# First stage of a fused graph kernel: weights centred on ScalarE, bias rows padded to 128 rows, and the quad sums of eight edge chunks made by TensorE

## The reference, cut to what matters

```python
xn = _layernorm(x)
# graph branch: edges are sorted by destination
out1 = segment_sum(edge_attr, dst); cnt = segment_sum(1, dst)
out2 = segment_max(edge_attr, dst); out3 = out1 / max(cnt, 1)
h = relu(concat([xn, out1, out2, out3, u]) @ W1 + b1) @ W2 + b2 + xn
# mixer
q, k, v = split(xn @ W_qkv + b_qkv)
q = q - mean(q); k = k - mean(k)          # the kernel centres the weights instead
q2, k2 = normalised squares of q and k    # k2 is normalised over all nodes
attn = v + q2 @ (k2.T @ v) / sqrt(N);  m = attn @ W_out + b_out
x = x + h + m
# then: layer norm, top half of the rows by a router, gelu MLP on them, scatter back
```

## Time and profile before

| | us |
|---|---|
| median of 3 runs | 1256.93 |
| lowest and highest of them | 1256.19, 1265.18 |
| the profiled execution | 1254.3 |
| its span, first to last instruction | 1252.5 |
| busy in the span: PE, DVE | 1062.0 (85%), 1016.3 (81%) |
| busy in the span: ACT, POOL | 483.2 (39%), 478.6 (38%) |
| mean granted TensorE clock | 0.914 of 2.4 GHz |

### The profile page before, as it was taken

How to read it: one execution, slowest core, us unless ns; L and a number is a source line. 1 busy time by engine, 2 the same in 40 slices (tenths; PEclk the granted TensorE clock), 3 DMA queues, 4 the chain that set the end, 5 groups by cost and what they waited for, 6 DMA issues and landing times. The chain is left out here.

```text
span 1252.5 us, 15955 instructions
## 1 busy us (share of the span) xinstructions
PE 1062.0 (85%) x4570; PEld 766.4 (61%) x4570; DVE 1016.3 (81%) x2429; ACT 483.2 (39%) x1438; POOL 478.6 (38%) x344
## 2 busy tenths in 40 slices
PE   3198999999993668699999999999999613899997
PEld 1044545555541445378888888888888503677775
DVE  6999999999999999568888998888895476545552
ACT  3346676677751234122233332223333220422430
POOL 0078831888000004485444456544420040133311
PEclk9599999999997788589999999999999855799998
DMA  8789999999998799533333344333321120111100
GB/s 304 300 314 340 345 370 356 348 348 348 353 320 318 295 414 366 189 103 118 128 125 108 111 147 136 125 126 129 94 75 45 42 68 8 27 43 40 52 23 19
DMA packets 96013, 235.53 MB, mean 188 GB/s; under 512 B 13703, under 2 KB 68764, under 8 KB 89682
## 3 DMA queue, kind: packets, MB, share of 16 engines
q1 hardware_dynamic: 49890, 156.61, 34.1%
q10 hardware_dynamic: 31248, 44.71, 10.0%
q0 software_dynamic: 14816, 33.53, 9.4%
HBM read 154.25 MB, written 80.55 MB: 187 GB/s over the span
## 5 line engine op out<-in xcount | busy, mean ns | idle before, releaser
L366 POOL DMA_INDIRECT graw<-in_edge_attr,ic x98 | 144.6, 1476 | 74.8 <-DVE ob L809 39.2
L806 DVE SCALAR_TENSOR_TENSOR ob<-ob,mQ,mx 128x96 f32<-128x96 f32 x392 | 122.1, 312 | 4.7 <-issue 0.4
L809 DVE SCALAR_TENSOR_TENSOR ob<-ob,kQ,xb 128x96 f32<-128x96 f32 x392 | 121.7, 311 | 0.0
L509 POOL DMA_INDIRECT near<-ends_d,blki x49 | 89.2, 1821 | 76.9 <-DVEq L715 62.2
L509 POOL DMA_INDIRECT near<-in_dst,rowi x49 | 87.8, 1792 | 57.8 <-DVEq L724 43.1
L1458 PE MATMUL psQ<-Wqk,xT 128*128 128x512 f32 (+1 forms) x196 | 102.2, 646 | 0.0
L1367 ACT ACTIVATE hT_hi<-psQ 128x512 fp32r<-128x512 f32 (+1 forms) x52 | 29.7, 572 | 182.8 <-PE psQ L1657 182.8
L794 DVE TENSOR_TENSOR xb<-xb 128x1536 f32<-128x1536 f32 x49 | 86.2, 1758 | 1.7
L792 DVE TENSOR_TENSOR mx<-xb 128x1536 f32<-128x1536 f32 x49 | 85.5, 1745 | 0.9
L2007 POOL DMA_INDIRECT out_x<-zo,lst x25 | 24.4, 977 | 129.4 <-DVE zo L2054 129.4
L61 PE MATMUL psF<-F2w,gT_hi 128*128 128x512 f32 (+1 forms) x175 | 67.0, 418 | 0.0
(11 more groups left out here) (462 smaller groups left out, 3201.9 us busy)
## 6 DMA issues: line engine op xcount, KB each, us to landing
xb<-in_edge_attr SPq DMA_DIRECT2D x49, 1536.0 KB, 10.4
scan_d<-ob SPq DMA_DIRECT2D x49, 768.0 KB, 5.7
yrow_d<-yr SPq DMA_DIRECT2D x48, 132.0 KB
xg<-in_x ACTq DMA_DIRECT2D x12, 512.0 KB, 10.7
xT_d<-xT ACTq DMA_DIRECT2D x12, 512.0 KB
base_d<-dcur ACTq DMA_DIRECT2D x12, 512.0 KB
qT_d<-qT ACTq DMA_DIRECT2D x12, 512.0 KB, 10.1
out_x<-xres SPq DMA_DIRECT2D x48, 128.0 KB
```

The costliest lines, as they stand in the source:

```text
L366: nc.gpsimd.indirect_dma_start(out=to.rearrange("p i f -> p (i f)"), out_offset=None, in_=raw_v, in_offset=bass.IndirectOffsetOnAxis(ap=ic ...
L509: nc.gpsimd.indirect_dma_start(out=near[:, t, :], out_offset=None, in_=table, in_offset=bass.IndirectOffsetOnAxis(ap=rows[:, t:t + 1], axi ...
L806: nc.vector.scalar_tensor_tensor(o[:, q, 0:EF], prev[:, 0:EF], mQ[:, bass.ds(c * TQ + q, 1)], mx[:, q, 0, :], ALU.min, ALU.max).then_inc(s ...
L809: nc.vector.scalar_tensor_tensor(o[:, q, EF:AGG], prev[:, EF:AGG], kQ[:, bass.ds(c * TQ + q, 1)], X[:, q, 0, :], ALU.mult, ALU.add).then_i ...
```

## The change

In the first stage:

- ACT centres the weights and biases (6 passes with a sum, 6 with a bias), after its segment searches and ahead of the square root of the variances. DVE keeps only the splitting of the bias (`query_bias`), which now stands before `variances`; `bias_row` moves to just after chunk 0. ACT issues its two small DMAs before the square root.
- `bqs`, `brow` and `one_r` get 128 partitions, set to zero by POOL at the start, and the two bias matmuls of a tile run over all 128 rows.
- For chunks 1 to 4 and 36 to 39, PE makes the quad sums: for each half of a chunk (four quads) four matmuls with the identity add the four edges of each quad, 384 columns wide, in PSUM (`quad_sums`, 8 matmuls a chunk). DVE leaves out L794 and L797 there and reads the sums from PSUM; it waits for `s_ps` before each half. In PE's order, the sums of chunk 1 stand before the node turns, those of chunks 2, 3 and 4 after the base of tiles (0,1), (0,3) and (1,2) of the turns, those of 36 after the last turn, those of 37 after the matmuls that make `M`, and those of 38 and 39 after attention groups 0 and 2.
- The block of factors moves from after chunk 39 to after chunk 36, the ends of segments to after chunk 38, SP's weight loads by one chunk forward, and the table `NORM` gets new places. The starts of segments move behind attention group 3 and use `psKx`.
- At the end of the stage, the four tail parts stand together behind the transposes into `psR`, and ACT issues the six loads of the node stage before its casts of the tail.

```diff
+SUMS_EARLY = (1, 2, 3, 4)
+SUMS_LATE = (36, 37, 38, 39)
-            bqs = sb("bqs", [2, 2 * NF], f32r)
+            bqs = sb("bqs", [P, 2 * NF], f32r)
 (brow and one_r likewise)
-                with sp.Fori(0, 10) as g:
+                with sp.Fori(0, 9) as g:
...
-                    if c == 40:
+                    if c == 39:
                         sp.wait_ge(s_at, 6 + KF)
                         sp.wait_ge(s_fs, TILES)
-                    if c in (40, 41):
+                    if c in (39, 40):
...
+                for m in (bqs, brow, one_r):
+                    nc.gpsimd.memset(m[:, :].bitcast(f32), 0.0).then_inc(s_id, 1)
...
-                def centre_weights():
+                def query_bias():
+                    dve.wait_ge(s_cw, 12)
+                    dve.wait_ge(s_id, 9)
...
+                    on_pe = c in SUMS
                     nc.vector.tensor_tensor(mx, xp[..0..], xp[..1..], ALU.max)
+                    if not on_pe:
                         nc.vector.tensor_tensor(xp[..0..], xp[..0..], xp[..1..], ALU.add)
                     nc.vector.tensor_tensor(mx[:, :, 0, :], mx[:, :, 0, :], mx[:, :, 1, :], ALU.max)
+                    if not on_pe:
                         nc.vector.tensor_tensor(X[:, :, 0, :], X[:, :, 0, :], X[:, :, 2, :], ALU.add)
...
+                        if on_pe and q % 4 == 0:
+                            dve.wait_ge(s_ps, SUMS.index(c) * 2 + q // 4 + 1)
+                        quad_sum = psS[c][q // 4][:, q % 4 * EF:(q % 4 + 1) * EF] if on_pe else X[:, q, 0, :]
...
-                NORM = {5: 0, 7: 1, 10: 2, 13: 3, 16: 4, 18: 5, 21: 6, 24: 7, 26: 8, 29: 9, 32: 10, 34: 11, 35: 12}
+                NORM = {6: 0, 9: 1, 11: 2, 14: 3, 16: 4, 19: 5, 21: 6, 24: 7, 26: 8, 29: 9, 31: 10, 33: 11, 34: 12}
                 edge_chunk(0, 0, 0)
+                bias_row()
                 stats_quarter(1)
                 stats_quarter(2)
+                stats(GROUPS, 1, LAST, xs[0], s_xs[0], 64)
+                query_bias()
                 variances()
-                centre_weights()
-                bias_row()
                 deviations()
...
-                    if c == 39:
+                    if c == 36:
                         (factors kcol and rq, then s_fac)
-                    if c == 39:
+                    if c == 38:
                         ends_of_segments()
...
+                for w_, m_, o_ in centred:
+                    nc.scalar.activation(o_, w_, ACT.Copy, scale=-1.0 / NF, accum_out=m_).then_inc(s_cw, 1)
+                for i, (w_, m_, o_) in enumerate(centred):
+                    act.wait_ge(s_cw, i + 1)
+                    nc.scalar.activation(w_, w_, ACT.Identity, bias=m_).then_inc(s_cw, 1)
...
-                for g in range(GROUPS + 1):
+                for g in range(GROUPS):
                     attention_rows(g, g % 4, g // 4 * 16)
                     weights(g)
+                attention_rows(GROUPS, 0, GROUPS // 4 * 16)
                 (the six loads of the node stage)
+                weights(GROUPS)
...
+                def quad_sums(c):
+                    pe.wait_ge(s_load[c % XB], c // XB * 16 + 16)
+                    for h in range(2):
+                        if c not in (SUMS_EARLY[0], SUMS_LATE[0]):
+                            pe.wait_ge(s_sum, (c - 1) * TQ + 4 * h + 5)
+                        for i in range(4):
+                            ins = nc.tensor.matmul(psS[c][h][:, 0:4 * EF], ident[:, :], xb[c % XB][:, 4 * h:4 * h + 4, i, :],
+                                                   start=(i == 0), stop=(i == 3))
+                        ins.then_inc(s_ps, 1)
...
-                    nc.tensor.matmul(o, one_r[0:2, 0:rows], bqs[0:2, :], start=True, stop=False)
+                    nc.tensor.matmul(o, one_r[:, 0:rows], bqs[:, :], start=True, stop=False)
 (brow likewise)
...
+                        if (g, t) in ((0, 1), (0, 3), (1, 2)):
+                            quad_sums({(0, 1): 2, (0, 3): 3, (1, 2): 4}[g, t])
...
-                tail_part(0)
-                tail_part(1)
                 pe.wait_ge(s_scan, 2)
                 (transposes into psR)
-                tail_part(2)
-                tail_part(3)
+                for i in range(4):
+                    tail_part(i)
```

More of the change, by code:

```diff
@@ L349, in build @@
             psW = psQ + psKx
+            psS = {c: psKx if c in SUMS_EARLY else [psR, psC] for c in SUMS}
             psA, psH, psO = psT, psQ + psKx, [psR, psC]
@@ L738, in rows_to_gather @@
                     dve.wait_ge(s_t, 1)
-                    step(nc.vector.tensor_copy(Sbeg[:, :], psR[:, 0:TILES]))
+                    step(nc.vector.tensor_copy(Sbeg[:, :], psKx[1][:, 0:TILES]))
                     step(nc.vector.tensor_scalar(a1[:, :], Sbeg[:, :], 3.0, None, ALU.add), False)
@@ L1126, in _ @@
                 nc.scalar.copy(wrb[:, :], psKx[1][:, 0:NF + 1]).then_inc(s_wrb, 1)
+                act.wait_ge(s_wload, 16 * 8)
+                centred = [(Wqk[:, c, h * NF:(h + 1) * NF], wm[:, 2 * c + h:2 * c + h + 1], xn[2][:, 2 * c + h, 0:NF]) for c in range(KF) for h in range(2)]
+                centred += [(bqk[0:1, h * NF:(h + 1) * NF], wm[0:1, 4 + h:5 + h], xn[3][0:1, h, 0:NF]) for h in range(2)]
+                for w_, m_, o_ in centred:
[3 more added lines that the diff above has]
+                    nc.scalar.activation(w_, w_, ACT.Identity, bias=m_).then_inc(s_cw, 1)
+                act.wait_ge(s_bw, 2)
+                act.dma_start(brow[1:2, :].bitcast(f32), brow_l[0:1, :].bitcast(f32)).then_inc(s_row, 16)
+                act.wait_ge(s_wq, 1)
+                act.dma_start(bqs[1:2, :].bitcast(f32), bqs_l[0:1, :].bitcast(f32)).then_inc(s_row, 16)
                 act.wait_ge(s_ln, 1)
                 nc.scalar.sqrt(sd[:, :], va[:, :]).then_inc(s_sqrt, 1)
-                act.wait_ge(s_wq, 1)
-                act.dma_start(bqs[1:2, :].bitcast(f32), bqs_l[0:1, :].bitcast(f32)).then_inc(s_row, 16)
-                act.wait_ge(s_bw, 2)
-                act.dma_start(brow[1:2, :].bitcast(f32), brow_l[0:1, :].bitcast(f32)).then_inc(s_row, 16)
                 act.wait_ge(s_ln, 2)
@@ L1467, in base @@
                     o = psC[0:rows, 0:NF]
-                    nc.tensor.matmul(o, one_r[0:2, 0:rows], brow[0:2, :], start=True, stop=False)
+                    nc.tensor.matmul(o, one_r[:, 0:rows], brow[:, :], start=True, stop=False)
                     for c in range(KF):
@@ L1515, in _ @@
                 pe.wait_ge(s_wrb, 3)
+                quad_sums(1)
                 pe.wait_ge(s_wq, 1)
@@ L1542, in _ @@
                 ins.then_inc(s_pt, 1)
+                pe.wait_ge(s_at, 4)
+                quad_sums(SUMS_LATE[0])
                 pe.wait_ge(s_at, 5)
@@ L1557, in _, with starts_of_segments @@
                 ins.then_inc(s_pt, 1)
-                pe.wait_ge(s_end, 1)
-                nc.tensor.matmul(psR[:, 0:TILES], shift[:, :], Eend[:, :], start=True, stop=False)
-                nc.tensor.matmul(psR[:, 1:TILES], corner[:, :], Eend[:, 0:TILES - 1], start=False, stop=True).then_inc(s_t, 1)
+                quad_sums(SUMS_LATE[1])
                 pe.wait_ge(s_at, 6 + KF)
+                def starts_of_segments():
+                    pe.wait_ge(s_end, 1)
+                    nc.tensor.matmul(psKx[1][:, 0:TILES], shift[:, :], Eend[:, :], start=True, stop=False)
+                    nc.tensor.matmul(psKx[1][:, 1:TILES], corner[:, :], Eend[:, 0:TILES - 1], start=False, stop=True).then_inc(s_t, 1)
                 def low_part(i):
@@ L1569, in low_part @@
                     pe.wait_ge(s_min, 4)
+                    if i == 3:
+                        pe.wait_ge(s_idx, 1)
                     if i >= 4:
@@ L1605, in _ @@
                     attention(g, g % 4, g // 4 * 16 + 16)
+                    if g in (0, 2):
+                        quad_sums(SUMS_LATE[2 + g // 2])
+                    if g == 3:
+                        starts_of_segments()
                     weights(g)
```

64 lines of the change are left out of this document (23 added, 41 removed).

## The result

The changed kernel is slower: 1311.14 us (median of 4, 1310.66 to 1312.15) against 1260.41 for the kernel before beside it (1256.19 to 1265.18); the ratio is 1.0406, 95% interval 1.036 to 1.0452. The profiled execution took 1310.66 us, its span 1308.9. I had forecast 1271, at most 1281. Most of the difference is one stall, and it doesn't always come: further down the same kernel takes 1259.8 us on each of two chips.

The account below looks back on a forecast made before the run. DVE's unbroken edge scan was taken as the bound, PE a close second. 1254.3 + 16.4 (early and late waits) - 1.8 (end of stage) = 1268.9 us profiled, 1271 as median; range 1255 to 1281.

Parts of the forecast that it names:

- Where DVE then waits: Chunks 1 to 4: DVE waits for PE's place in the turns, some 28 us; chunk 4 ends at 106.9, before 91.8.
- the case to which I gave 0.42: Whole kernel: time the same as before, within about 1% (12.6 us); chance 0.42.
- PE reaches its quad sums sooner: Rival: first tile starts at 52, chunk 4 ends at 99.8, no late chunk waits; 1250 to 1261 us, chance 0.2.
- DVE's own work: Chunks with PE sums: 2.5 us shorter, eight times, 20 us; PSUM reads free; centring saves 4.25; chunk 1 starts at 51.3.
- when PE can begin: Chunk 1's sums on PE, first at half clock: halves at 54.3 and 57.2; node turns begin at 57.2.
- The waits of chunks 2 to 4: First carries wait on PE: halves at 68.5 and 71.3, 81.6 and 84.4, 102.1 and 105.0; some 13 us before chunk 4.
- The bias rows: Node tiles on PE: bias matmuls over 128 rows save 0.5 us a tile (0.4 to 0.6), leaving 3.55 us.
- the rival, no gain: Bias matmuls: padding saves nothing, a tile stays at 4.2 us; 1282 us (1277 to 1286), chance 0.17.
- The late four: Chunks 36 to 39: 36 without wait, 38 and 39 wait 2 and 6 us; 39 ends at 433.2, 16.4 later than before.
- The end of the stage: Tail and node-stage loads: `xTs_hi` starts 1.8 us earlier, at 522.4; 1.8 us gained (0 to 2.5).

Follow-up runs that it names:

- the control: The changed kernel unaltered, run on chip E beside two other versions: 1259.77 us, 1.0036 of the kernel before.
- two rows: The changed kernel with the bias matmuls over two rows again instead of 128, on chip E: 1269.25 us, 1.0125 of the kernel before.
- padding alone: The kernel before with only the bias rows padded to 128 rows, on chip B: 1254.22 us, 0.9982 of the kernel before.
- four others: Chip A: changed kernel without early sums 1247.41 us, with later gathers 1271.84, with two-row bias 1272.30; kernel before with DVE idled 1299.13.

## Why the prediction was wrong

The direction was right, the time was 40 us too low, and the runs show two errors that partly hide each other.

**The step that failed against the result** is "Where DVE then waits", in its chunk 3: "halves at 81.6, 84.4; ends at 86.3". By the records PE had them at 84.4 and 87.0 (that it began on them at 81.6 has to do with the late signals too: in the control without a stall it begins at 76.6), but DVE could use them only at 102.3 and 124.6. No term and no rival of the prediction has signals of PE that arrive late; the sum took it that work recorded as done releases its waiter, and nothing in the rows spoke against that. At chunk 5 it makes 49.7 us (152.7 against 103.0 in the control on chip E), which is nearly all of the 51 us between the two times.

**Where there is no stall**, the forecast of 1271 was 11 us too high, and 1.0036 is within 1%, the case to which I gave 0.42. The profiled control took 1260.5 against the 1268.9 of my sum; 4 us of that are there at chunk 5 and 9 at chunk 40. By its time, and by chunk 4 ending at 103.0, before 104, this is the rival "PE reaches its quad sums sooner" (0.2, 1250 to 1261), but not by its mechanism: the first tile starts at 57.5 and not at 52, and chunk 39 still waits 5.9 us. The control, step by step, chunk starts on DVE:

```profile
51.68 1.76 DVE L782 TENSOR_TENSOR mx<-xb 128x1536 f32<-128x1536 f32 x1
...
71.71 1.75 DVE L782 TENSOR_TENSOR mx<-xb 128x1536 f32<-128x1536 f32 x1
...
79.58 0.32 DVE L802 SCALAR_TENSOR_TENSOR ob<-ob,mQ,mx 128x96 f32<-128x96 f32 x1 [5.13 <-PE psKx L1451]
...
83.88 1.75 DVE L782 TENSOR_TENSOR mx<-xb 128x1536 f32<-128x1536 f32 x1
...
98.76 0.32 DVE L802 SCALAR_TENSOR_TENSOR ob<-ob,mQ,mx 128x96 f32<-128x96 f32 x1 [12.14 <-PE psKx L1451]
...
103.00 1.75 DVE L782 TENSOR_TENSOR mx<-xb 128x1536 f32<-128x1536 f32 x1
```

- **DVE's own work, when PE can begin**: right. Chunk 1 at 50.9 and 51.7 (51.3 forecast), the halves of chunk 1 taken up at 54.4 and 57.1 (54.3, 57.2), PSUM reads free: the carry takes 0.31 us from either source.
- **The waits of chunks 2 to 4**: right in kind and order, the longest 12.1 us before chunk 4 (some 13), too long in sum. Chunk 5 starts at 103.0 and not 106.9. The term that was mis-sized is PE's pace. A half of the sums takes 2.58 us and not 2.8 to 2.9: a call of 384 columns is 0.64 (5.16 for eight, from 64.52 to 69.68 on PE), where I had scaled 0.72 from the 0.96 of a longer one. So DVE waits 0.5 us and not 1 for each second half. And a tile's matmuls follow each other faster than I took from one bias matmul (next point).
- **The bias rows**: the rival, no gain, is refuted by 9.5 us on one chip, where I had put the difference at 11. The term that was mis-sized is the saving of a tile. Control, then two rows, first and second tile on PE:

```profile
57.48 0.50 PE L1476 MATMUL psQ<-bqs,one_r 128*128 128x512 f32 x1 [0.24 <-ACT xT L1162]
57.81 1.88 PE L1478 MATMUL psQ<-Wqk,xT 128*128 128x512 f32 x4
59.13 0.68 PE L1488 MATMUL psC<-brow,one_r 128*128 128x256 f32 x1
...
61.08 0.48 PE L1476 MATMUL psQ<-bqs,one_r 128*128 128x512 f32 x1
```

```profile
56.52 0.49 PE L1476 MATMUL psQ<-bqs,one_r 2*128 2x512 f32 x1 [0.24 <-ACT xT L1162]
56.94 1.98 PE L1478 MATMUL psQ<-Wqk,xT 128*128 128x512 f32 x4
58.86 0.38 PE L1488 MATMUL psC<-brow,one_r 2*128 2x256 f32 x1
...
60.87 0.50 PE L1476 MATMUL psQ<-bqs,one_r 2*128 2x512 f32 x1
```

The distances of the starts give it: 3.60 us a tile against 4.35, so 0.75 saved and not 0.5. In which call it lies they don't tell, because a recorded start can lie before the work: the full bias call of 256 columns starts at 59.13, and the last of the four `Wqk` matmuls, which follow each other by 0.43, at 59.10. PE's signals at the end of `psQ` and of `psC` do tell. In the second tile 2.17 and 1.41 us pass up to them in the control (61.12, 63.29, 64.70), and 2.56 and 1.80 with two rows (60.74, 63.30, 65.10). So each two-row call costs 0.39 us more than a full one, that of 512 columns and that of 256 alike; I had 0.25 for each. The weight loads (PEld) show where it goes. The load of the second bias call, control and two rows:

```profile
59.10 0.19 PEld L1488 LDWEIGHTS psC<-brow,one_r 128*128 128x128 f32 x1 [0.24 <-issue]
```

```profile
58.85 0.18 PEld L1488 LDWEIGHTS psC<-brow,one_r 2*128 2x128 f32 x1 [0.76 <-issue]
```

In the control it runs beside the last `Wqk` matmul (59.10); with two rows it starts only with its own matmul (58.86). So does the first load behind a two-row call (56.94, with its matmul at 56.94; in the control 57.59, before 57.81). Two loads of 0.18 to 0.19 us in the open at each two-row call are about the 0.39. By the Trainium skill, page "TensorE: Matmul & The Clock Gate", section "LDWEIGHTS (loading the stationary operand)", a load's time goes by its columns and not by its rows, from which I had made the rival of no gain. The loads here agree with it, 0.18 us for two rows and 0.19 for 128. The prediction said that rows 6 and 7 disagree with it, but they are rows of matmuls; what costs is not the length of a load but that it no longer runs beside a matmul.
- **The late four**: 36 and 37 without loss and 39 with 6 us were right. The control:

```profile
387.91 1.75 DVE L782 TENSOR_TENSOR mx<-xb 128x1536 f32<-128x1536 f32 x1
...
406.46 0.32 DVE L802 SCALAR_TENSOR_TENSOR ob<-ob,mQ,mx 128x96 f32<-128x96 f32 x1 [0.39 <-PE psR L1451]
...
419.91 0.32 DVE L802 SCALAR_TENSOR_TENSOR ob<-ob,mQ,mx 128x96 f32<-128x96 f32 x1 [5.89 <-PE psR L1451]
...
424.15 1.75 DVE L782 TENSOR_TENSOR mx<-xb 128x1536 f32<-128x1536 f32 x1
```

Chunks 36 to 39 with the factors take 36.2 us; the forecast has 41.0 (392.2 to 433.2), the kernel before 39.2. Chunk 38 waits 0.4 and 0.3 us and not 2, and chunk 37, which I had at 7.9 us, takes 6.5. So they gain 3 us where I had them lose 1.8. In the kernel without early sums they lose 1.8 us at chunk 40 beside the one without any sums (41.0 against 39.2 from the start of 36): there chunk 37 waits 3.8 us. I take it that how much they give depends on the lead that the turns have over the scan; where the 3.8 come from I did not follow further.
- **The end of the stage**: `xTs_hi` starts 18.4 us after the scan in the control (530.92 less 512.56; 17.8 forecast, 19.6 before). But the term stands at the wrong place. With padding alone `xTs_hi` comes 7.8 us earlier than before, because PE's granted clock is 0.87 instead of 0.50 of 2.4 GHz between 504 and 520 us, so that a pair of tail matmuls takes 1.02 instead of 1.91; and yet the span is only 0.9 shorter. PE's next waits in that run and the last of them in the kernel before:

```profile
533.58 1.51 PE L1639 MATMUL psT<-ident,agg 128*128 128x128 f32 x6 [5.13 <-DVE agg L928]
...
539.02 0.77 PE L50 MATMUL psQ<-aggT_hi,W1f_hi 128*128 128x512 f32 x1 [1.49 <-DVE tailT L939]
```

```profile
539.15 0.77 PE L50 MATMUL psQ<-aggT_hi,W1f_hi 128*128 128x512 f32 x1 [1.50 <-DVE tailT L936]
```

PE waits for DVE's aggregates 12 to 17 us after `xTs_hi`, and these follow the scan and its repair, not `xTs_hi`. I should have asked what is late next.

Of the change without the stall, then: the centring gives 3.5 us at chunk 1 and what follows the scan some 3 at the end (the kernel without sums is 7.3 us faster than the kernel before on B), the padding nothing by itself, the early sums cost 12.4 (1259.8 against 1247.4, on two chips), and the late ones lie between a gain of 3 and a loss of 2.

**What stays open.** What holds PE's signals on the one kind of chip, and whether it is the chip, the time of the run or the recording that makes the kind. For the gathers speaks that in all three executions profiled with the stall it ends at 130.1 to 130.8 us, 7 to 8 us after the last gather was issued; against them as a sufficient cause, that on the other chips they run beside an idle DVE without effect, and that on chip C they did so beside a working one. Whether a chip of that kind stalls without the gathers was not tried: the four runs with the gathers moved were all without the mark in the trace and without the stall, and so were all with two-row bias matmuls.

## What to carry to other kernels

Work that is moved from a busy in-order engine to another costs the waiting of the first for the second's place in its own queue: 2.5 us saved a chunk, up to 12 us waited, and moving one such piece of work forward by two tiles gave back 7 us of 7. Give away only what the other engine does before it is asked. And measure the control on every chip before an experiment is read against it: one run of the unchanged kernel refuted what four others had seemed to show.

## What the hardware showed that I had not expected

- One kernel has two times: 1259.8 us on two chips and 1311 on two occasions, one of them on a third chip, with most executions of an occasion within 2 us of each other, while the kernel before differs between these occasions by only 5 to 8 us in its medians (1254.5 and 1255.5 against 1260.4 and 1262.4).
- On the two occasions with 1311 us PE's signals were recorded up to 43 us after the recorded end of their matmuls.
- A two-row bias matmul costs 0.39 us more than one over 128 rows, at 512 columns and at 256: by the rows, its load and the next one don't run beside a matmul.
